# Masks of every other head written by ScalarE into the score bank, and contexts laid out with features first by the host

## The reference, cut to what matters

```python
# x: (8, 256, 256), ctx_1024: (8, 256, 256), D = 256, H = 16 heads of 16 features
def mha(q, k, v, ..., mask):                       # block 0, twice: self-attention, then attention to the context
    Q, K, V = (q @ wq + bq), (k @ wk + bk), (v @ wv + bv)      # each split into 16 heads
    att = einsum('bhqd,bhkd->bhqk', Q, K)
    att = where(mask == 0, -1e9, att)
    att = softmax(att, axis=-1)
    return einsum('bhqk,bhkd->bhqd', att, V) @ wo + bo
x1 = mha(x, x, x, ..., tgt_mask);        x2 = layer_norm(x + x1)
x3 = mha(x2, enc_out, enc_out, ..., src_mask);  x4 = layer_norm(x2 + x3)
x5 = relu(x4 @ ff_w1 + ff_b1) @ ff_w2 + ff_b2;  return layer_norm(x4 + x5)
...
x = x + tanh(g_xattn[0]) * block0(layernorm(x), ctx_1024, masks)     # the above
x = x + tanh(g_ffn[0])   * experts(layernorm(x))                     # 2 of 8 experts for each row
x = x + tanh(g_xattn[1]) * rotary_attention(layernorm(x), ctx_1024)  # no 2-D mask; keys and values from the context
x = x + tanh(g_ffn[1])   * experts(layernorm(x))                     # 1 of 8 experts for each row
```

## Time and profile before

| | us |
|---|---|
| median of 3 runs | 1367.42 |
| the profiled execution | 1368.68 |
| its span, first to last instruction | 1366.9 |
| TensorE busy | 1199.9 |
| VectorE busy | 781.0 |
| ScalarE busy | 569.9 |
| GpSimd busy | 556.7 |
| exponentials of the first attention (256), ScalarE | 151.4 |

### The profile page before, as it was taken

The page is one execution under the profiler, slowest core; times in us unless marked ns, Lnnn a source line. Parts: engine busy times, 40 slices in busy tenths (PEclk is TensorE's granted clock), DMA queues, the critical chain, the costliest instruction groups (busy, mean ns, idle before and its releaser), DMA issues. The chain is left out here.

```text
span 1366.9 us, 27489 instructions
## 1 busy us (share of the span) xinstructions
PE 1199.9 (88%) x8469; PEld 968.4 (71%) x8524; DVE 781.0 (57%) x2994; ACT 569.9 (42%) x1404; POOL 556.7 (41%) x927
## 2 busy tenths in 40 slices
PE   4599999999998999899999999447888868689996
PEld 3367677777755788789999999434556645689995
DVE  4587777777773378865333333136787876532231
ACT  2156566666655223233333333112455545233331
POOL 3334454453534235545333333144554433433331
PEclk9799999999999999999999999876899999799998
DMA  4766664635420991123222222187453695511110
GB/s 107 167 139 161 140 162 101 121 84 110 101 48 2 304 285 33 47 30 46 32 40 40 36 37 35 17 188 162 105 105 86 144 279 186 186 33 46 40 35 6
DMA packets 116679, 137.66 MB, mean 101 GB/s; under 512 B 25627, under 2 KB 102953, under 8 KB 111628
## 3 DMA queue, kind: packets, MB, share of 16 engines
q1 hardware_dynamic: 101304, 106.73, 33.1%
q0 software_dynamic: 15232, 29.17, 9.3%
HBM read 102.51 MB, written 35.97 MB: 101 GB/s over the span
## 5 line engine op out<-in xcount | busy, mean ns | idle before, releaser
L768 DVE CUSTOM_DVE_ANT_0 att_masked_scores<-att_S,Bm 128x256 bf16<-128x256 f32 x512 | 192.4, 419 | 66.9 <-PE att_S L511 52.8
L648 ACT ACTIVATE att_PT<-att_T 128x512 f32<-128x512 f32 x256 | 151.4, 595 | 86.3 <-PE att_T L530 77.6
L2432 ACT ACTIVATE moe_hT<-moe_H,moe_b 128x128 f32<-128x128 f32 x312 | 89.2, 369 | 170.1 <-PE moe_H L2345 168.9
L2357 PE MATMUL moe_Z<-moe_W,moe_hT 128*128 x624 | 141.6, 380 | 0.8 <-DVE moe_z L2657 0.8
L2520 POOL DMA_INDIRECT x<-Y,X x39 | 63.7, 1634 | 154.7 <-DVE Y L2668 150.4
L2357 PEld LDWEIGHTS moe_Z<-moe_W,moe_hT 128*128 128x128 f32 x624 | 115.5, 190 | 15.5 <-issue 1.2
L511 PE MATMUL att_S<-L_KS,L_QS 96*128 96x256 bf16 x512 | 99.7, 277 | 18.3 <-DMA L_KS<-att_k_dram 13.3
L530 PE MATMUL att_T<-L_QS,L_KS 99*128 99x256 bf16 x512 | 98.6, 273 | 4.6 <-issue 2.1
L2345 PEld LDWEIGHTS moe_H<-moe_aT,ff_w 128*128 128x128 f32 x832 | 96.8, 192 | 4.0 <-issue 2.1
L2345 PE MATMUL moe_H<-moe_aT,ff_w 128*128 128x128 f32 x832 | 97.2, 275 | 2.3 <-DVE X L2652 1.7
L1805 DVE TENSOR_REDUCE out_mx<-out_S 128x2 f32<-128x512 f32 x128 | 85.1, 684 | 24.6 <-PE out_S L1223 24.0
(11 more groups left out here) (455 smaller groups left out, 2527.1 us busy)
## 6 DMA issues: line engine op xcount, KB each, us to landing
moe_W<-in_L_ffn_W SPq DMA_DIRECT2D x16, 1024.0 KB, 13.6
L_W<-in_L_ffn_W POOLq DMA_DIRECT2D x12, 1024.0 KB, 10.7
att_q_dram<-att_pq SPq DMA_DIRECT2D x16, 384.0 KB, 4.5
att_k_dram<-att_pk SPq DMA_DIRECT2D x16, 384.0 KB, 2.8
L_QS<-att_q_dram SPq DMA_DIRECT2D x16, 384.0 KB, 4.9
L_KS<-att_k_dram SPq DMA_DIRECT2D x16, 384.0 KB, 8.1
L_QS<-att_q_dram SPq DMA_DIRECT2D x16, 256.0 KB, 5.6
L_KS<-att_k_dram SPq DMA_DIRECT2D x16, 256.0 KB, 8.5
```

Of the source, the lines that this page charges most:

```text
L648: nc.scalar.activation(PT[:, h % 8, :], bankT[h % 2][:, :], ACT.Exp).then_inc(exp_done, 1)
L768: ins = nc.vector.tensor_tensor_reduce(masked_scores[:, h % 2, u, :], bankS[h % 2][:, u * SEQ:(u + 1) * SEQ], masks[m // B][0][:, u * SEQ: ...
L2357: ins = nc.tensor.matmul(bankZ[:, 0:D], eT[:, s % 2, f * P:(f + 1) * P], w2e[:, f, :], start=(f == 0), stop=(f == NF - 1))
L2432: ins = nc.scalar.activation(eT[:, s % 2, g * P:(g + 1) * P], bankH[half][:, f * P:(f + 1) * P], ACT.Relu, bias=b1[:, bass.ds(e * NF + g, 1)])
```

## The change

Two things are done together.

First, in the first attention, the mask of an odd head is no longer added by a matmul. After the exponential of odd head h ScalarE waits until that exponential is complete and copies the mask, 128x512 in bf16, into the same bank (bankT[1], `seed`). TensorE's `scores_T` of head h + 2 waits for this copy, leaves its mask matmul out, and its two score matmuls add to what lies in the bank (start=False). Head 1 of the first unit keeps its matmul, and there is no copy after the last odd head: 127 of 256 masks move.

Second, the host hands over the context with features first. It is loaded as it is used, so `turn_context`, `bring_context` and cT are gone in both attentions: eight turns and copies in each. The bank order loses these tasks. In the first attention the context comes in eight transfers in place of one. In the second, the load of the first expert, which overwrites the context's place, waits for the last keys and values.

```diff
-TASKS = {... 12: (("z", -1),), 14: (("c", 4),), 15: (("o", 2),)}
+TASKS = {... 12: (("z", -1),), 15: (("o", 2),)}
...
-    sp.dma_start(mem["C"][:, :, :], mem["ctx_in"].rearrange("b (u p) d -> p (b u) d", p=P)).then_inc(mem["c_in"], 16)
+    for n in range(B):
+        sp.dma_start(mem["C"][:, n, :, :], mem["ctx_in"][n].rearrange("(c p) t -> p c t", p=P)).then_inc(mem["c_in"], 16)
...
             def keys(m):
-                pe.wait_ge(*taken("c" if cross(m) else "x", m))
-                product("k", m, w_of(m)["wk"], cT if cross(m) else xT)
+                if cross(m):
+                    pe.wait_ge(mem["c_in"], 16 * B)
+                else:
+                    pe.wait_ge(*taken("x", m))
+                product("k", m, w_of(m)["wk"], C[:, m % B, :, :] if cross(m) else xT)
...
-                pe.wait_ge(exp_done, H * m + h + 1)
                 dst = bankT[h % 2]
-                nc.tensor.matmul(dst[:, :], identb[:, :], masks[m // B][1][:, :], start=True, stop=False)
+                if h % 2 and (m, h) != (0, 1):
+                    pe.wait_ge(seeded, seed_no(m, h))
+                else:
+                    pe.wait_ge(exp_done, H * m + h + 1)
+                    nc.tensor.matmul(dst[:, :], identb[:, :], masks[m // B][1][:, :], start=True, stop=False)
...
+            def seed(m, h):
+                act.wait_ge(exp_done, H * m + h + 3)
+                layer = (m if h + 2 < H else m + 1) // B
+                nc.scalar.activation(bankT[1][:, :], masks[layer][1][:, :], ACT.Copy).then_inc(seeded, 1)
...
                     if has(b):
                         exps(b, h)
+                        if h % 2 and (b, h) != (M - 1, H - 1):
+                            seed(b, h)
...
-FILL = ("c", 0), ("k", 0), ("v", 0), ("x", 0), ("q", 0), ("c", 1), ("k", 1), ("v", 1), ("x", 1), ("q", 1), ("c", 2), ("k", 2), ("v", 2)
+FILL = ("k", 0), ("v", 0), ("x", 0), ("q", 0), ("k", 1), ("v", 1), ("x", 1), ("q", 1), ("k", 2), ("v", 2)
...
-                pe.wait_ge(*taken("c", m))
-                product("k", m, w["wk"], cT)
+                pe.wait_ge(mem["c_in"][m], 16)
+                product("k", m, w["wk"], C[m])
...
             def first_expert():
-                pool.wait_ge(*full("c", M - 1))
+                pool.wait_ge(*full("k", M - 1))
+                pool.wait_ge(*full("v", M - 1))
...
+    given["c_ctx_1024"] = np.swapaxes(given.pop("ctx_1024"), -1, -2)
```

More of the change, by code:

```diff
@@ L596, in _ @@
                         project_out(b - 1)
-                    if h == 14 and has(b + 4) and cross(b + 4):
-                        turn_context(b + 4)
                     if h in TURN_AT and 0 <= turning < QUADS * M:
@@ L678, in _ @@
                         bring_rows(b + 4)
-                    if h == 14 and has(b + 4) and cross(b + 4):
-                        bring_context(b + 4)
                     g = QUADS * b + (h - 5) // 4
@@ L1373, in _ @@
             queries(0)
-            turn_context(1)
             keys(1)
@@ L1418, in _ @@
                         project_out(b - 1)
-                    if h == 14 and has(b + 4):
-                        turn_context(b + 4)
                     if b == M - 1 and h == 11:
```

67 lines of the change are left out of this document (17 added, 50 removed).

## The result

The changed kernel takes 1346.77 us (median of 5 runs, 1345.34 to 1353.81) beside 1367.42 of the kernel before (1361.56 to 1370.19) on the same chip: a ratio of 0.9859, 95% interval [0.9836, 0.9883]. The forecast was 1343.5 in a range of 1336 to 1356. The profiled execution is the longest of the five, 1353.81 us with a span of 1352.0.

A forecast was written before the change was run, and what follows sets the result against it. TensorE was taken to bound the first attention's beats. Gains of 20.9 us there and 3.4 in the second attention sum to 24.3, from 1368.68 to 1344.4, predicted as a median of 1343.5; range 1337 to 1350, 1336 to 1356 with two rivals.

The forecast's parts named there:

- two small stalls: Each first-attention beat: TensorE waits for exponentials queued behind ScalarE's copies, 0.16 us at head 4, 0.21 at head 8.
- the 4 us that hung on it: First attention: with a mask copy of 0.49 us or less both stalls go, 4 us more gain.
- the walk: Step-by-step schedule of TensorE and ScalarE through one first-attention beat, giving 21.96 + 0.37 = 22.33 us.
- The two beats from 87.4 to 132.7: Early first-attention beats without a turned context, counted at 1.36 us gain each.
- my first rival: First attention: stacked keys become the bound; half of 12 beats stalling 1.6 us gives 1353; chance 14%.
- The last stretches: End of first attention: gains of 0.65 us from 373.89 and 0.7 from 394.32; drain 0, with -1 to +1.
- The first stretch: First attention from 68.9 us, where VectorE sets the pace; gain put at 0.4 us.
- The 2.1 of the fill: Second attention's fill: keys of unit 2 can start where the turned context did, saving 2.1 us.
- The 0.85 and 0.4: Second attention: context turned before the first beat saves 0.85 us; of four in the beats one counts, 0.4.
- second rival: First attention: ScalarE's order costs more, by dearer copies or longer waits for exponentials; 1351.5 at the dear bound; chance 11%.
- third rival: First attention: holes and late loads lower TensorE's clock; a third of the stage lower gives 1403; chance 6%.
- fourth rival: First attention: mask matmuls were hidden under weight loads or waits, so time stays near 1364; chance 5% with near-no-change cases.

The follow-up runs named there:

- the later loads: Changed kernel with the loads of the context's second half and of later weights issued behind the stacked rows instead of ahead; 1343.82 us, ratio 0.9830.
- The bias first: Changed kernel with GpSimd's addition of the output's bias moved ahead of gain and shift; 1349.32 us, ratio 0.9879.
- the two conversions one head later: Changed kernel with ScalarE's first conversion of queries moved behind head 2's exponential, that of keys behind head 6's; 1346.53 us, ratio 0.9861.
- the context alone: Kernel before with only the features-first context, all masks staying on TensorE; 1356.16 us, ratio 0.9936.
- three more masks: Changed kernel with the two conversions one head later, plus ScalarE copying masks behind heads 0, 4 and 12; 1351.73 us, ratio 0.9878.
- all masks: Changed kernel with ScalarE copying masks behind even heads' exponentials too, nearly all heads; 1374.88 us, ratio 1.0058.
- copied twice: Changed kernel with each mask copied twice by ScalarE, the second copy waiting for the first; 1376.70 us, ratio 1.0085.
- the masks alone: Kernel before with only the odd heads' masks moved to ScalarE, contexts turned as before; 1353.35 us, ratio 0.9914.

## Why the prediction was right, and where its terms were off

The time lies 3.3 us (6.3 in the second session) above the forecast and inside its range. The mechanism was right in the main: TensorE sets the beat, work taken off it shortens the beat, and ScalarE's order gives two small stalls back. The sum was 24.3 us, and the medians give 20.7 and, in the second session, 1365.85 - 1349.77 = 16.1. The last step of the sum has a slip: 1344.4 less 1.3 is 1343.1. Several terms were off, most of them too high, and about 2 us of the gain came from the clock before the beats begin, which no term had; that the first median comes so near is partly luck.

- **The price of the copy and its place**: 0.60 forecast, 0.602 measured; 0.63 behind its exponential and 0.54 ahead of the next. The Trainium skill, ScalarE: Activation LUTs, section "Step-by-step: what each stage is for", gives a write to PSUM the lower latency. The copy's 0.602 beside the 0.591 of the exponentials, which write the other memory, does not show it, and the 4 us that hung on it did not come.
- **The steady beat**: 24.13 to 22.33 forecast, 22.57 measured in six beats, 6 x 0.24 = 1.4 us less gain. The beat between the two late ones and the one behind them take more, 22.88 and 23.11 us in the first profile and 22.87 twice in the second: another 1.2 us less. With the later loads they too take 22.56 and 22.57. Both stalls stood where the walk put them, within 0.02 us. The step that failed is "VectorE frees each score bank at least 0.08 before TensorE wants it". It missed one bank by 0.20, behind an addition that waits for three instructions of GpSimd in a row. The walk left GpSimd out altogether; but its chain of 3.9 us starts when VectorE has normed a unit's rows, and VectorE does this late, since an instruction of 0.19 us is held for 1.18 beside GpSimd's addition. The new beat put these two at the same time. The bias first leaves this hold in place, and did not give the 0.20 back; the two conversions one head later take it away, and the late scores with it.
- **The two beats from 87.4 to 132.7**: 2.7 forecast, 0.75 measured (45.25 to 44.51 and 44.49). They are not steady beats with less in them: the first has no output projected, 1.73 us of TensorE that would let ScalarE catch up. In both profiles of the changed kernel TensorE waits 0.55 us there for a copy, and in the next beat 0.53 for VectorE's maxima, where the kernel before has neither wait. To value them like a steady beat was wrong by 2.0 us.
- **The stacked rows**: my first rival, given 14%, was true in part. Waits of 1.66 and 1.50 us (1.02 and 1.63 in the second profile) came at beats 3 and 5. The walk's release-to-scores of 12.0 was about right (138.23 to 150.82, 12.6), but the median landing of 8.5 us was the wrong number for beats that also load weights and context: there it took 14.2 from release to scores (138.23 to 152.48). The two stretches with these waits gave -0.2 and -0.3 us, where 0.65 and 1.8 were forecast: 2.9 us less, with the piece at the lower clock in one profile of two. The later loads gave 364.7 - 361.8 = 2.9 us back, and 3.9 behind the first stretch. The rival's price of 9.6 for half of the beats was too high: only the beats with other loads were hit.
- **The last stretches** gave more, 1.7 us against 0.65 for the one from 373.89, since its own wait shrank from 2.16 and 2.03 to 1.36. The one from 394.32 gave 1.9 against 0.7: the clock was granted at 0.92 and 0.95 in it before, behind those waits, and at 1.00 after; at 1.00 the context alone takes 17.46 and the change 17.04, so 0.4 is the masks' and 1.5 the clock's. The drain took 34.5 and 33.7 us instead of 33.0 twice, 1.1 more, just outside the forecast's 0 with -1 to +1.
- **The first stretch**: 0.4 forecast; 18.51 and 20.01 before, 20.20 twice after. The 18.51 was chance, and no gain is left.
- **The second attention**: 3.4 forecast, 2.0 measured (489.0 in the mean of the three profiles that turn a context, 487.0 in that of the eleven that don't). The 2.1 of the fill came to the letter at its step: the keys start 3.58 us behind the queries (911.62 to 915.20), before 5.68 (923.99 to 929.67). From these queries to the first maxima the gain is larger, 8.5 to 9.1 us in the eleven beside 10.8 to 12.2 in the three; the stage ahead, which the change leaves alone, scatters by 2 us. The 0.85 and 0.4 did not show: from the first to the last maxima the means are 193.1 and 193.2 us, with single profiles from 190.6 to 195.9.
- **ScalarE's order dearer** (second rival): no, but close by: each further copy in a beat costs (three more masks, all masks, copied twice).
- **The clock** (third rival): it stayed at 1.00 in all steady beats with three late steps of 0.14 to 0.22 us. From 87 us to the drain it fell once, behind the 1.50 at 199.12 (0.56 from there to 203 us), but not behind the 1.66 at 152.48, nor behind any wait of the second profile. So not the small holes but a late load costs clock, and not always.
- **The masks hide nothing** (fourth rival): refuted by the 10.1 us of the masks alone.

These terms make 13.2 of the 20.9 us of the first attention, and 2.0 of 3.4 of the second. Added to that is an earlier start of the beats: 66.7 and 66.9 beside 68.9 and 68.4, 1.9 us in the mean. Eleven of the twelve profiles with either part of the change have it, the one with three more masks (68.5) does not. The traces show where it comes from, in the stretch from 55 to 60 us, before and after:

```profile
55.00:60.00 5.00, 4.17 (x13) 2.36 (x11) 3.18 (x17) 0.63 (x1) 3.13 (x14) 0.50 0.63 107
55.00:60.00 5.00, 3.49 (x17) 2.42 (x16) 3.64 (x16) 0.93 (x2) 3.32 (x13) 0.87 0.50 89
```

The three profiles with a late start are those with the lower clock here, 0.50, and 0.72 to 0.77 from 60 to 65 us; the eleven others were granted 0.85 to 1.00 and then 1.00. A projection at 60.46 takes 2.91 us to the next start in the kernel before, and the same one at 59.43 takes 1.73 in the changed kernel. So the earlier start is TensorE's clock. The kernel with three more masks holds both halves of the change and has the lower clock all the same, so the change does not settle it; what does stays open. The three parts make 17.1 us; the spans of the two profiles each differ by 15.7 in the mean, the medians by 16.1 and 20.7, and what lies between is scatter that no run here explains.

## What to carry to other kernels

Work moved off the bounding engine is worth its full price only while every other engine keeps its turn at each hand-over: walk all the queues that touch the shared banks, not just the one that gets the work, look which instructions of VectorE and GpSimd come to lie side by side, and do it once for the steady loop and once for each beat that lacks a task. When a loop gets shorter, look at its transfers in the beats where they have company: there the landing time of the median row does not hold. And two cheap moves of order (two conversions one head later, loads behind the rows that are waited for) took 6.5 us more from the attention (364.7 to 358.2), half of the change's own 13.2, while three more moved masks and an earlier bias gave nothing or cost time.

## What was not expected of the hardware

VectorE and GpSimd hold each other up: two normalisations of 128x256 take 0.71 us alone, 0.91 where GpSimd's addition of 128x512 ends in them, and 1.78 where it runs its 1.32 us beside them; and the maxima's small instruction takes 1.18 instead of 0.19 beside an addition of 1.16. This is the lock that the Trainium skill, SBUF — State Buffer, section "SBUF: two separate sides", describes, in which the later of the two engines waits for the whole instruction of the other; the traces agree, in the order of ends too (GpSimd at 293.17, VectorE at 293.33).

Three issues of stacked rows took 1.26 us without the weights' loads and 2.13 us with them: the issuing becomes slower too, not only the landing. And ScalarE starts an exponential 0.26 us behind an output copy that lasts 0.36 (283.65 to 283.91), so it overlaps its successor by 0.10 us, as the exponential of 0.60 does whose successor starts 0.50 behind it.
